# Keys and values beside the first attention, two additions of a router on GpSimd, and edge lists and x asked for earlier

## The reference

```python
def gt_layer(edge_index, embeds, qT, kT, vT, ln_s, ln_b):
    rows, cols = (edge_index[0], edge_index[1])
    q = (embeds[rows] @ qT).reshape(-1, HEAD, hd)
    k = (embeds[cols] @ kT).reshape(-1, HEAD, hd)
    v = (embeds[cols] @ vT).reshape(-1, HEAD, hd)
    expAtt = jnp.exp(jnp.clip(jnp.einsum('ehd,ehd->eh', q, k), -10.0, 10.0))
    attNorm = jax.ops.segment_sum(expAtt, rows, num_segments=n)[rows]
    ...  # sum of weighted v by rows, plus embeds, layernorm
def linear_attention(x, w_qkv, w_out, b_out):
    q, k, v = ...                      # x @ w_qkv
    q = jax.nn.elu(q) + 1.0
    k = jax.nn.elu(k) + 1.0
    kv = jnp.einsum('bnhd,bnhm->bhdm', k, v)
    z = 1.0 / (jnp.einsum('bnhd,bhd->bnh', q, k.sum(axis=1)) + EPS_ATTN)
    return jnp.einsum('bnhd,bhdm,bnh->bnhm', q, kv, z).reshape(B, N, D) @ w_out + b_out
# router
e = jax.nn.leaky_relu(a_src[src] + a_dst[dst], negative_slope=0.2)
ee = jnp.exp(e - e_max[dst])           # then sums of ee and of ee * h[src] by dst
# together
xn = _layernorm(x)
x = x + gnn(xn, edge_index, ...) + mix(xn, ...)
x = x + ffn(_layernorm(x), ...)        # 4 experts, the best 2 weighed by the router
```

## Time and profile before

| | |
|---|---|
| median of 3 runs | 9530.21 us (9505.88 to 9555.25) |
| the profiled execution | 9526.39 us, its span 9524.7 us |
| mean granted TensorE clock | 0.710 |
| busy: PE, PEld, DVE, ACT, POOL | 5350.2, 4186.2, 5845.2, 1041.7, 5064.7 us |
| share of the span | 56%, 44%, 61%, 11%, 53% |
| `enter` | 1058.80 to 1355.90 us of the span |
| first attention, second attention | 1355.90 to 4054.90, 4148.30 to 6738.50 |
| `neighbour_sum` | 8776.00 to 9382.00 |

### The profile page before, as it was taken

How to read it: one execution, slowest core, us unless ns; L and a number is a source line. 1 busy time by engine, 2 the same in 40 slices (tenths; PEclk the granted TensorE clock), 3 DMA queues, 4 the chain that set the end, 5 groups by cost and what they waited for, 6 DMA issues and landing times. The chain is left out here.

```text
span 9524.7 us, 116553 instructions
## 1 busy us (share of the span) xinstructions
PE 5350.2 (56%) x27325; PEld 4186.2 (44%) x27325; DVE 5845.2 (61%) x16179; ACT 1041.7 (11%) x3289; POOL 5064.7 (53%) x5138
## 2 busy tenths in 40 slices
PE   5868675555555555545444444444657777776331
PEld 3535444444444444435444444444435555454221
DVE  7878436666666666666555555555655555556776
ACT  0000230000000000010000000000212222221220
POOL 2323126666666666646666666666155555555441
PEclk7555787777777777776777677777668888787555
DMA  0000223333333333334333333333322222222326
GB/s 22 3 11 3 48 55 103 104 100 104 101 104 103 102 101 103 97 93 111 109 106 108 104 106 107 106 105 104 104 42 49 45 47 50 47 49 51 86 64 155
DMA packets 489594, 765.03 MB, mean 80 GB/s; under 512 B 119849, under 2 KB 349726, under 8 KB 488946
## 3 DMA queue, kind: packets, MB, share of 16 engines
q0 software_dynamic: 202656, 454.22, 18.4%
q1 hardware_dynamic: 277798, 291.62, 11.7%
q10 hardware_dynamic: 8492, 11.74, 0.5%
HBM read 692.20 MB, written 64.96 MB: 79 GB/s over the span
## 5 line engine op out<-in xcount | busy, mean ns | idle before, releaser
L663 POOL DMA_INDIRECT att_kv_e<-kv,gnn_idx x3336 | 3402.1, 1020 | 2167.1 <-issue 968.5
L737 PE MATMUL att_ps_sum<-att_vals,att_hot 128*125 128x136 f32 x6672 | 1329.2, 357 | 2468.8 <-DVE att_vals L785 2100.7
L737 PEld LDWEIGHTS att_ps_sum<-att_vals,att_hot 128*125 128x125 f32 x6672 | 1133.8, 246 | 2643.1 <-DVE att_vals L785 2240.1
L663 POOL DMA_INDIRECT max_rows<-rows,gat_idx x1128 | 1065.0, 944 | 960.9 <-ACT src_sb L1753 451.2
L726 PE MATMUL att_ps_q<-qs,att_hot_t 125*128 x6672 | 1287.5, 337 | 136.9 <-issue 122.9
L802 DVE TENSOR_TENSOR acc<-acc,att_ps_sum 125x136 f32 x1668 | 488.6, 293 | 1214.3 <-remote 760.9
L726 PEld LDWEIGHTS att_ps_q<-qs,att_hot_t 125*128 125x128 f32 x6672 | 1134.9, 245 | 223.9 <-issue 219.5
L761 DVE TENSOR_TENSOR att_prod<-att_ps_q,att_kv_e 128x512 f32<-128x512 f32 x834 | 569.9, 683 | 906.9 <-remote 771.2
L1773 DVE CUSTOM_DVE_ANT_0 max_junk<-max_far,max_ps_b 125x256 bf16<-125x256 bf16 x2256 | 803.5, 417 | 490.2 <-PE max_ps_b L1739 202.3
L748 ACT ACTIVATE att_vals<-att_clipped 128x32 f32<-128x32 f32 x834 | 191.2, 229 | 4902.6 <-DVE att_clipped L793 2417.9
L1739 PE MATMUL max_ps_b<-max_a_t,pick_head 12*125 12x512 bf16 x1128 | 382.9, 456 | 443.6 <-ACT max_a_t L1748 366.2
(11 more groups left out here) (447 smaller groups left out, 7024.5 us busy)
## 6 DMA issues: line engine op xcount, KB each, us to landing
att_local<-gnn_loc_rows SPq DMA_DIRECT2D x834, 128.0 KB
att_kv_e<-kv,gnn_idx POOLq DMA_INDIRECT x3336
max_local<-gat_loc_rows SPq DMA_DIRECT2D x282, 128.0 KB
gs_local<-gat_loc_rows SPq DMA_DIRECT2D x141, 256.0 KB, 3.3
outs<-ex_y SPq DMA_DIRECT2D x25, 896.0 KB
max_rows<-rows,gat_idx POOLq DMA_INDIRECT x1128
ans_late<-outs SPq DMA_DIRECT2D x11, 896.0 KB
ans_early<-outs SPq DMA_DIRECT2D x8, 896.0 KB
```

What stands on the lines that cost most here:

```text
L663: pool.indirect_dma_start(rows(j, e), None, source, bass.IndirectOffsetOnAxis(ap=g.idx[:, t:t + 1], axis=0))\
L737: ins = pe.matmul(ps_sum[j % 2][0:NODE_TILE, p * 256:p * 256 + SUMS], hot[:, j, PAIR * p + e, :], vals[:, j % 2, PAIR * p + e, :], start=e ...
```

## The change

1. **Edge lists.** The tensors of both graphs' lists now exist from the start of `place`, and all four lists are asked for, each in two transfers, by SP in the block of `sort_constants`. The two tails of `gat` stay in `sort_edges`.
2. **x.** Its ten transfers are issued in `unpack`, between the load of `gnn_lists` and the store of `gnn_loc_rows`.
3. **`enter`** loses everything of keys and values (L1272, L1286, L1324, L1327, L1340, L1214, L1219, and two of the ten weights). Each turned tile is also stored to DRAM (`x_turned`), from a ring of four instead of two.
4. **`Keys`**, a new class, does that work beside the first attention, one node tile every eight steps: for tile t in step 8t + 4 SP loads the turned tile, + 6 TensorE multiplies, + 7 ScalarE copies, + 8 and + 10 VectorE, + 9 ScalarE's exp, + 11 TensorE sums.
5. **`Mix`** moves from beside the first attention to beside the second. `Shift` is gone; its add is one more operation of `Mix`. Its buffer of squares is now the one of `xr`, with two more waits.
6. **`neighbour_sum`.** `sums` and `less` go from VectorE to GpSimd. The values they need are kept four steps instead of two, the one-hots four instead of six, and the lags on all engines are new.

The diff, cut to its core:

```diff
 def sort_constants(nc, st, pairs, graphs):
...
     with semaphores(nc, ["sort_const_steps"]) as (ready,), nc.Block() as block:
+        @block.sync
+        def _(sp):
+            for g in graphs:
+                assert g.parts == NODE_TILE
+                for tensor, edges in ((g.key_sb, g.key), (g.other_sb, g.other)):
+                    deal(sp, tensor[:, 0:g.full], edges[0:g.parts * g.full].rearrange("(p n) -> p n", p=g.parts), g.lists_in)
...
 def sort_edges(nc, c, s, g):
...
-            for tensor, edges in ((key_sb, g.key), (other_sb, g.other)):
-                sp.dma_start(tensor[:, 0:g.full], edges[0:full].rearrange("(p n) -> p n", p=p)).then_inc(m["edges_in"], 16)
             if g.rest:
...
-            dve.wait_ge(m["edges_in"], 64 if g.rest else 32)
+            dve.wait_ge(g.lists_in, 64)
+            if g.rest:
+                dve.wait_ge(m["edges_in"], 32)
...
-def unpack(nc, st, c, g):
+def unpack(nc, st, c, g, also=None):
...
             sp.dma_start(lists[:], g.table.rearrange("(q p l) -> p q l", p=LANES, l=LANES)).then_inc(m["lists_in"], 16)
+            if also is not None:
+                also(sp)
             sp.wait_ge(m["row_ready"], 1)
...
-class Shift:
...
+class Keys:
...
+    def load(self, sp, n):
+        t = self.tile_at(n, 4)
+        if t is not None:
+            wait(sp, self.m["kv_ps"], t - 1)
+            sp.dma_start(self.xT[:, t % 2].rearrange("p c n -> p (c n)"), self.x_turned[t])\
+                .then_inc(self.x_in[t % 2], 16)
     def vector(self, dve, n):
...
+        t = self.tile_at(n, 8)
+        if t is not None:
+            dve.wait_ge(m["k_copied"], t + 1)
+            wait(dve, m["k_ready"], t)
+            dve.tensor_scalar(self.k_exp[:], self.k_raw[:], 0.0, None, ALU.min).then_inc(m["k_min"], 1)
+
+        t = self.tile_at(n, 10)
+        if t is not None:
+            dve.wait_ge(m["k_exped"], t + 1)
+            wait(dve, m["summed"], t)
+            dve.scalar_tensor_tensor(out=self.k[:], in0=self.k_raw[:], scalar=0.0, in1=self.k_exp[:],
+                                     op0=ALU.max, op1=ALU.add).then_inc(m["k_ready"], 1)
...
+    def tensor(self, pe, n):
+        m = self.m
+        t = self.tile_at(n, 6)
+        if t is not None:
...
+            pe.wait_ge(self.x_in[t % 2], 16 * (t // 2 + 1))
+            wait(pe, m["v_copied"], t)
+            for ch in range(KC):
+                kv_of = pe.matmul(self.ps_kv[0:NODE_TILE, :], self.xT[:, t % 2, ch, :], self.wkv[:, ch, :],
+                                  start=ch == 0, stop=ch == KC - 1)
...
+        t = self.tile_at(n, 11)
+        if t is not None:
+            pe.wait_ge(m["k_ready"], t + 1)
+            pe.wait_ge(m["v_copied"], t + 1)
+            for ch in range(KC):
+                sum_of = pe.matmul(self.ps_sum[ch][:, 0:LANES + 1], self.k[:, ch * LANES:(ch + 1) * LANES],
+                                   self.v[:, ch, :], start=t == 0, stop=t == self.tiles - 1)
...
     def scalar(self, act, n):
...
+        t = self.tile_at(n, 7)
...
+            act.activation(self.k_raw[:], self.ps_kv[0:NODE_TILE, 0:GIN], ACT.Identity, scale=at2(self.ratio, t))\
+                .then_inc(m["k_copied"], 1)
...
+        t = self.tile_at(n, 9)
...
+            act.activation(self.k_exp[:], self.k_exp[:], ACT.Exp).then_inc(m["k_exped"], 1)
...
 class Mix:
...
+            dve.wait_ge(m["turned"], min(t + 2, self.tiles))
             dve.tensor_tensor(self.square[:], h, h, ALU.mult).then_inc(m["squared"], 1)
...
         t = self.tile_at(n, 17)
         if t is not None:
+            dve.wait_ge(m["stepped"], t + 1)
+            dve.tensor_tensor(X[:, t], X[:, t], self.shift[:], ALU.add).then_inc(m["shifted"], 1)
...
 def enter
...
-            for i in range(chunks):
-                a = slice(i * CHUNK, (i + 1) * CHUNK)
-                deal(sp, X[:, a], source[:, a], x_in[i])
...
+            for n in range(tiles + 1):
+                if n < tiles:
+                    sp.wait_ge(m["turned_sb"], n + 1)
+                    sp.dma_start(x_turned[n], xT[:, n % TURNED].rearrange("p c n -> p (c n)"))\
+                        .then_inc(saved[n % TURNED], 16)
+                if n:
+                    sp.wait_ge(m["kv_copied"], n)
+                    sp.nop(nofuse=True)
+                    deal(sp, rows[n - 1], kv_sb[:, (n - 1) % 2, :], stored[(n - 1) % 2])
...
+                wait(act, m["projected"], t - TURNED + 1)
+                wait(act, saved[t % TURNED], 16 * (t // TURNED))
+                act.copy(xT[:, t % TURNED], turned_ps.rearrange("p (c n) -> p c n", c=KC)).then_inc(m["turned_sb"], 1)
...
-            steps(pool, [(0, weigh), (-1, rest_of), (-2, low)])
+            def sums(k, r, j):
+                pool.wait_ge(m["info"], k + 1)
+                wait(pool, m["exps"], (k - 4) + 1)
+                pool.tensor_tensor(e_sb[:, k % 4], src_of(k)[:, :, FE:FE + FH], info[:, k % 4, :, 0:FH], ALU.add)\
+                    .then_inc(m["sums"], 1)
+
+            def less(k, r, j):
+                pool.wait_ge(m["leaky"], k + 1)
+                pool.tensor_tensor(e_sb[:, k % 4], e_sb[:, k % 4], info[:, k % 4, :, FH:2 * FH], ALU.subtract)\
+                    .then_inc(m["less"], 1)
+            steps(pool, [(0, sums), (-1, less), (-2, weigh), (-3, rest_of), (-4, low)])
...
-            steps(pe, [(1, load_tiles), (-3, add_up), (1, fetch)])
+            steps(pe, [(1, load_tiles), (-5, add_up), (1, fetch)])
...
-            steps(act, [(-1, high), (-2, middle), (0, exps)])
+            steps(act, [(-3, high), (-4, middle), (-1, exps)])
...
-            steps(dve, [(0, gather_info), (-4, add_sum(0)), (0, sums), (-4, add_sum(1)), (0, leaky), (-4, add_sum(2)),
-                        (2, near_hot), (-3, load_tile(0)), (-4, add_sum(3)), (0, less), (1, one_hot), (-3, load_tile(1)),
-                        (-3, load_tile(2)), (-3, load_tile(3))])
+            steps(dve, [(0, gather_info), (-6, add_sum(0)), (-1, leaky), (-6, add_sum(1)), (2, near_hot), (-6, add_sum(2)),
+                        (-5, load_tile(0)), (-2, one_hot), (-6, add_sum(3)), (-5, load_tile(1)), (-5, load_tile(2)),
+                        (-5, load_tile(3))])
```

242 lines of the change are left out of this document (110 added, 132 removed).

## The result

| | before | change |
|---|---|---|
| median | 9530.1 us (6 runs, 9505.9 to 9555.3) | 9474.4 us (6 runs, 9455.7 to 9491.3) |
| ratio | | 0.9942, 95% interval 0.9926 to 0.9959 |
| profiled execution, span | 9526.4, 9524.7 us | 9473.6, 9471.2 us |
| mean granted clock | 0.710 | 0.707 |

A forecast was written before the change was run, and what follows sets the result against it. Entry was taken as bound by its loop, attention by GpSimd's gathers, the router's sum by VectorE's register loads. Terms -14.4 - 10.7 + 8 - 120 + 25 + 0 - 31 = -143 us gave 9387 us; range 9325 to 9475.

The forecast's parts named there:

- What bounds the kernel: Whole kernel: entry by its 5.36 us loop, attention by GpSimd's gathers, router's sum by VectorE's four register loads.
- Edge lists: Sort and router's list: asking for lists early removes waits, -14.4 and -10.7 us.
- x's chunks: Start of entry: begins 19 us later behind x's transfers, weights then arrive sooner; net +8 us.
- `enter`'s loop: Entry: without keys and values the period falls from 5.36 to 2.81 us; -120 us after an allowance.
- that rival: Entry: TensorE's clock falls to 1.2 GHz, period 4.7, 95 us of gain lost, 9482 us; chance 0.07.
- Keys beside the first attention: First attention: keys and values cost +25 us, between 16 by VectorE's share and 109 by TensorE's.
- The mixer moves: Attentions: the mixer goes from first to second with all its work and the shift's add; 0, within 10 us.
- Router's sum: Router's `neighbour_sum`: VectorE's new order shortens the period from 4.08 to 3.83 us; -31 us.
- a port: Router's sum: port shared by GpSimd and VectorE takes the gain back, period stays 4.08, 9418 us; chance 0.13.
- keys cost as much as the mixer did: First attention: keys cost 110 us instead of 25, total 9472 us; chance 0.11.
- Slower than before: First attention: keys' chain hides nothing, 5.7 us a tile, 285 us instead of 25, 9647 us; chance 0.03.
- the sum's own bounds: Whole kernel: bounds on keys, router, start and attention stalls together reach from 9325 to 9440 us.

The follow-up runs named there:

- chip A: Kind of chip where the kernel before takes 8260 to 8270 us; the change took 8105.7 against 8260.4 there, ratio 0.9814.
- part 3: Reading of time lines, nothing changed: in the kernel before's first attention ScalarE's exp started over 1 us late in 73 steps, 524 us late in all.
- chip C: Kind of chip where the kernel before takes 9519 to 9530 us, as in the first comparison; the change's ratio there was 0.9942.
- m1_bare: Changed kernel with keys, values, mixer and shift left out beside both attentions, on chip C: attentions 2559.1 and 2574.3 us.
- m2_new_mix_first: Kernel before with the change's mixer beside the first attention and nothing beside the second, on chip C: first 2739.5, second 2559.6 us.
- m3_best: Change with x's loads split around the start of `enter` and the router's two additions back on VectorE, on chip C: 9466.5 against 9518.8 us, 0.9930.
- chip B: Kind of chip where the kernel before takes 9705 us; its bare attentions took 2662 and 2666 us.
- short products: Change with the keys' products cut to 8 columns after the first tile, waits and other engines' work kept, on chip B: first attention 2668.3 us.
- g2_no_sums: Change without the router's sum's two additions on any engine, on chip C: router's sum 595.7 us, against 595.4 with them on GpSimd.

## Why the prediction was right and wrong

- **What bounds the kernel**: right for `enter`. For the attentions it was half right. I read "stretches in which slots are not given back" as part of the kernel; on chip A there are none, and the gathers' 5.2 us a step (4 x 1.31) are nearly the stage's time, 5.3. Where they do occur, a late signal of TensorE goes with them (part 3).
- **Edge lists**: right, 25.5 us against 25.1.
- **x's chunks**: right. Start 17.0 later (19 forecast), weights 8.5 us after the block's start (10), net 4.8 lost (8).
- **`enter`'s loop**: right, period 2.91 for 2.81; the stage lost 130 us (131). The clock stood at 0.92, so that rival did not come, at a lower busy share than before. By the Trainium skill ("TensorE: Matmul & The Clock Gate", What's actually happening) it could have fallen; the trace does not show it.
- **Keys beside the first attention**: the step that failed. Of the 87 us that are missing, 63 are this term's; the mixer's move has 17, the router's sum 18, and the other stages give back about 10. "By VectorE's share keys cost 16 us, by TensorE's 109 ... I take +25" gave 88 on the chips of the first comparison (71 to 97 over five traces), near the end I had put aside. Three things were wrong in it. The price of the mixer was taken as 2699 - 2590 = 109, but the subtrahend held the shift, and the bare attention takes 2559: the mixer costs 148. And the reason for VectorE's share (GpSimd waits for its weighing, TensorE has slack) was not borne out: keys add 26 us of VectorE where the old mixer adds 254, a tenth, and cost six tenths of what it does. And TensorE's 180 us for the keys added up single durations that overlap: busy time in the earlier trace rows is 95.3 + 35.6 = 131 us, and beside the attention keys add 107 where the old mixer adds 184. By TensorE's share of the right base keys would cost 107/184 x 142 = 83 us. On chip C the prices do go with TensorE's work (by `m1_bare`, `m2_new_mix_first` and `m3_best` 97 us for 107 of it, 180 for 192), on chip B they do not (15 for 123, 71 for 247), so whether TensorE's work or the chain through the engines makes the price is not shown; short products took 9 us off on chip B, and were not run on C.
- **The mixer moves, 0 within 10**: right for the place (180 and 177), wrong for the new form. In the first comparison's traces the second attention grew by 159 us where the first had lost 142: 17 us, of which scatter may be 15.
- **Router's sum, -31**: mis-sized and for a wrong reason. It gave 12.8. The period went to 3.95 instead of 3.83, since the three loads begin 2.0 us behind the gather and not 1.88; so 0.13 us a step came instead of 0.25, 18 us, and filling and draining the longer pipeline took 5 of them (4 forecast). The credit belongs to the new order and lags: without the two additions on any engine nothing changed. The load at 9054.7 that I took for the one ahead of the wide one-hot is the first of the three behind it. By the Trainium skill ("Perfetto Trace Analysis", Optimizing Scalar/DVE Operations) the move may gain nothing; it gained nothing, but `g2_no_sums` shows no cost of a port either, and the place of the register loads in VectorE's order is what I read as the reason.
- **The rivals**: nearest was "keys cost as much as the mixer did", 9472 against 9474 measured, by 88 where it had 110, helped by a router's sum 18 short. It had 0.11 and should have had far more: both of its ends were rows, and I chose between them by an argument. "Slower than before" did not come, though in the first comparison the two attentions cost 105 us of the 168 from which it decides.
- **The size as a whole**: on chip A the change took 155 us off, where the sum said 143; that so near a hit is in part luck, since two terms missed in opposite directions: keys cost 7 to 9 us there, not 25, and the router's sum gave 13 to 14, not 31. That 9474 us lie inside the range, by less than 1 us, is owed to its having been drawn over most of the case of keys; by the sum's own bounds it would have ended at 9440.

## What to carry to other kernels

Work beside a loop has no price of its own: the same keys and values cost 7 to 9, 15 and 88 us on three kinds of chip. Where the gathers alone set the pace they were nearly free; where the ring of slots runs dry they were not, and the bare loop's time does not tell how dear they are (15 us over 2662, 88 over 2559). Price it against the bare loop, not against the loop with something else beside it, and if the ends of the bound are 16 and 109, forecast the middle. Before crediting a gain to an engine that was relieved, ask for the run in which the work is left out altogether; here it changed nothing, and the order and lags around it did. And where a profile names no releaser, read in the kernel's text what the engine waits for: here two engines that seemed to stand still for nothing waited for one semaphore of TensorE.
